# Decay and keys of the gated linear attention read from PSUM, the value gates multiplied in two halves, and the order of turns redrawn

## The reference

```python
# gla, H = 4 heads, 16 key and 32 value channels each
q = (x @ Wq); k = (x @ Wk); v = (x @ Wv)
gk = log_sigmoid(x @ gk_w1 @ gk_w2 + gk_b2) / 16
def step(S, qkvg):
    S = jnp.exp(gt)[..., None] * S + kt[..., None] * vt[..., None, :]
    ot = jnp.einsum('bhk,bhkv->bhv', qt, S)
# experts: the values are gated by expert and summed
xv = jnp.einsum('bsd,hedp->bshep', x, v_w)
v = jnp.einsum('bshep,bshe->bhsp', xv, gate_v)
```

## Time and profile before

| | before |
|---|---|
| median of 3 runs | 1421.68 us (1418.91 to 1423.92) |
| the profiled execution | 1440.95 us, span 1439.6 us |
| busy: TensorE, VectorE | 1271.5 us (88%), 1019.2 us (71%) |
| busy: ScalarE, GpSimd | 738.1 us (51%), 675.4 us (47%) |
| mean granted TensorE clock | 0.951 |

### The profile page before, as it was taken

How to read it: one execution, slowest core, us unless ns; L and a number is a source line. 1 busy time by engine, 2 the same in 40 slices (tenths; PEclk the granted TensorE clock), 3 DMA queues, 4 the chain that set the end, 5 groups by cost and what they waited for, 6 DMA issues and landing times.

```text
span 1439.6 us, 43040 instructions
## 1 busy us (share of the span) xinstructions
PE 1271.5 (88%) x18034; PEld 1014.5 (70%) x18034; DVE 1019.2 (71%) x2038; ACT 738.1 (51%) x2084; POOL 675.4 (47%) x549
## 2 busy tenths in 40 slices
PE   5576877999989999799999899979998899979887
PEld 3353566877777678578777778857787688867775
DVE  4758778877796877767688877887667676755334
ACT  5577865656554572445665367425673246323111
POOL 3445436673463446455556354445625464333500
PEclk9799989999999999999999999999999899989998
DMA  5101064743466347356566456744556465545642
GB/s 195 45 16 63 1 200 132 240 144 131 145 196 222 102 146 249 105 173 200 193 200 191 130 180 212 221 146 154 173 168 197 145 227 196 172 170 199 240 132 79
DMA packets 90721, 231.43 MB, mean 161 GB/s; under 512 B 9377, under 2 KB 15649, under 8 KB 90401
## 3 DMA queue, kind: packets, MB, share of 16 engines
q1 hardware_dynamic: 90384, 228.09, 48.6%
q10 hardware_dynamic: 144, 0.59, 0.1%
HBM read 225.50 MB, written 3.15 MB: 159 GB/s over the span
## 4 chain that ended last, share of the span: by engine, by line
PE 43%; DVE 10%; issue 3%; ACT 1%; DMA 1%; POOL 1%; DVEq 0%; ACTq 0%; POOLq 0%
PE bank L968 10%; PE bank L921 9%; PE bank L831 5%; PE bank L958 3%; PE bank L939 2%; PE bank L616 2%; DVE kv L1154 2%; PE bank L949 1%; PE bank L932 1%; PE bank L651 1%; PE bank L675 1%; DVE dy L1238 1%; DVE ogate L1401 1%; PE bank L711 1%; PE bank L661 1%
## 5 line engine op out<-in xcount | busy, mean ns | idle before, releaser
L1795 POOL TENSOR_TENSOR vgate<-vgate,xT 128x1024 f32<-128x1024 f32 x128 | 309.1, 2419 | 149.8 <-DMA vgate<-gates 149.6
L921 PE MATMUL bank<-wv,vgate 128*128 128x128 f32 x2048 | 261.5, 283 | 0.5 <-DVE state L1354 0.3
L921 PEld LDWEIGHTS bank<-wv,vgate 128*128 128x128 f32 x2048 | 251.0, 198 | 9.7 <-issue 3.9
L968 PE MATMUL bank<-ogate,wo 128*128 128x256 f32 x1024 | 254.1, 393 | 2.7 <-DVE ogate L1401 2.6
L968 PEld LDWEIGHTS bank<-ogate,wo 128*128 128x128 f32 x1024 | 195.5, 197 | 37.0 <-issue 10.6
L1401 DVE TENSOR_TENSOR ogate<-ogate,bank 128x1024 f32<-128x1024 f32 x128 | 153.4, 1209 | 37.5 <-PE bank L958 31.6
L1758 POOL TENSOR_TENSOR kv<-kv,gqk 128x512 f32<-128x512 f32 x64 | 84.8, 1326 | 125.0 <-DVE kv L1154 125.0
L1690 ACT ACTIVATE mprob<-bank,mmin 128x256 f32<-128x256 f32 x128 | 59.3, 469 | 138.7 <-DVE mmin L1390 138.5
L1512 ACT ACTIVATE prob<-prob,mx 128x128 f32<-128x128 f32 (+1 forms) x256 | 95.9, 376 | 57.7 <-DVE mx L1095 57.0
L1741 POOL TENSOR_TENSOR rot<-rot 128x512 f32<-128x512 f32 x64 | 83.5, 1305 | 86.1 <-DVE rot L1071 85.9
L1753 POOL TENSOR_TENSOR prob<-prob,rsum 128x256 f32<-128x256 f32 (+1 forms) x64 | 60.4, 943 | 130.7 <-DVE rsum L1098 130.5
(11 more groups left out here) (236 smaller groups left out, 2602.1 us busy)
## 6 DMA issues: line engine op xcount, KB each, us to landing
vgate<-gates SPq DMA_DIRECT2D x128, 512.0 KB, 4.3
ogate<-gates SPq DMA_DIRECT2D x128, 512.0 KB, 4.5
wv<-in_wv_moe SPq DMA_DIRECT2D x128, 256.0 KB, 4.6
wo<-in_wo_moe SPq DMA_DIRECT2D x128, 256.0 KB, 4.8
kv<-values SPq DMA_DIRECT2D x128, 128.0 KB
local<-in_local SPq DMA_DIRECT2D x1, 1715.0 KB, 9.6
wqkv<-in_wqkv SPq DMA_DIRECT2D x2, 768.0 KB, 6.5
x<-in_x SPq DMA_DIRECT2D x8, 128.0 KB, 7.9
```

What stands on the lines that cost most here:

```text
L921: i = nc.tensor.matmul(out[:, n * D:(n + 1) * D], xg[:, e, n * P:(n + 1) * P], m.wv[slot][:, e, :], start=(q, n, e) == (0, 0, 0), stop=(q, ...
L968: i = nc.tensor.matmul(out[:, 0:T], m.wo[slot][:, e, :], cg[:, e, :], start=(h, q, e) == (0, 0, 0), stop=(h, q, e) == (MH - 1, 1, EQ - 1))
L1795: tt(gate, gate, spread(m.xT[b % 2][:, :], 1, EQ), ALU.mult).then_inc(s.vgated, 1)
```

## The change

- `gqk` on ScalarE copies only the queries, to a tile `gq`. The keys stay in the bank.
- `gkv` on VectorE takes the keys from the bank. It waits for the decay instead of for the bank's release.
- The last step of `gz` on ScalarE writes the decay into the first half of that same bank, over the queries that have been copied out; it waits for that copy.
- `gmul` on VectorE reads the decay from the bank. Behind its last round the bank is released, by a semaphore instruction that waits for those scans. The bank is thus held from `gqk` to the last scan.
- `vgate` on GpSimd issues two instructions on 128x512 in place of one on 128x1024; the semaphore rises behind the second.
- All five tables of turns and the table of banks are drawn anew, with as many steps as before.

```diff
@@ VectorE
         v.wait_ge(s.kv_in[slot], 32 * use)
-        v.wait_ge(qk.emptied, qk.use)
-        v.chain(tt(kv[:, :, :], kv[:, :, :], spread(m.gqk[:, 1, :], 1, 2), ALU.mult))
+        v.wait_ge(s.gdecay, nth("gz", b))
+        v.chain(tt(kv[:, :, :], kv[:, :, :], spread(filled(qk)[:, T:2 * T], 1, 2), ALU.mult))
 
     def gmul(b, j):
-        kv = m.kv[kv_of(b, j)[0]]
+
+        kv, qk = m.kv[kv_of(b, j)[0]], banks.of("gqk", b)
         v.settle()
         v.wait_ge(s.gdecay, nth("gz", b))
         for n in range(2):
-            i = nc.vector.tensor_tensor_scan(kv[:, n, :], m.ge[:, :], kv[:, n, :], 0.0, ALU.mult, ALU.add)
+            i = nc.vector.tensor_tensor_scan(kv[:, n, :], qk.ap[:, 0:T], kv[:, n, :], 0.0, ALU.mult, ALU.add)
         i.then_inc(s.gscan, 1)
+        if j == GJ - 2:
+            v.wait_ge(s.gscan, nth("gmul", b, j))
+            nc.vector.sem_inc(qk.emptied, 1)
@@ ScalarE
     def gqk(b):
         bank = banks.of("gqk", b)
-        act(m.gqk[:, :, :], split(filled(bank), n=2), ACT.Copy).then_inc(bank.emptied, 1)
+        act(m.gq[:, :], filled(bank)[:, 0:T], ACT.Copy).then_inc(s.gq, 1)
...
         a.wait_ge(s.gmin, nth("gz", b))
-        act(m.ge[:, :], ge, ACT.Exp, scale=1.0 / 16.0).then_inc(s.gdecay, 1)
+        a.wait_ge(s.gq, nth("gqk", b))
+        act(banks.of("gqk", b).ap[:, 0:T], ge, ACT.Exp, scale=1.0 / 16.0).then_inc(s.gdecay, 1)
@@ GpSimd
-        tt(kv, kv, spread(m.gqk[:, 0, :], 1, 2), ALU.mult).then_inc(s.gmul, 1)
+        tt(kv, kv, spread(m.gq[:, :], 1, 2), ALU.mult).then_inc(s.gmul, 1)
...
-        tt(gate, gate, spread(m.xT[b % 2][:, :], 1, EQ), ALU.mult).then_inc(s.vgated, 1)
+        half = EQ // 2
+        for e in range(0, EQ, half):
+            i = tt(gate[:, e:e + half, :], gate[:, e:e + half, :], spread(m.xT[b % 2][:, :], 1, half), ALU.mult)
+        i.then_inc(s.vgated, 1)
@@ the third line of BANK_TURNS
-    "52736573726571316576523572135723156213523521572156315373523271537153715231623125321574271546713546317243617274"
+    "01501416046156051601016016540154065140652140625061562145615426142164242160240240624053045364526164564561245621"
```

More of the change, by code:

```diff
@@ L123 @@
[L123 to L128 removed]
+    "aaaaaaaaabbabaXGGGGbabbbaaabaabGaaabbbbbGcaabcbGbbbccbbGcGaabbabGaacaaacGGGbaGcbacbbcaaabbbGaabbGaaabbabbGbcab"
@@ new lines @@
+    "cbGbGbbcacbbaacabbzbGCcCaaAFGcaabbACGGabGccVacAVzVAAaAbbbPabPbbAbbaabaVcGVAAcVAaaFacaPAbFbAGPVAPVbACFVCaAaaPAA"
+    "DbGPbbAVbbPcbcVVAbbaAAbCaAcDaVADDcaGAADVADVDcaAGVDAADDAaPbbDAPDbDAaFPDDGAaaPADPDPDDGGGDAGVDDaPDVbbbbDDAcbbDAcD"
+    "DFbbDAFbDDacDAaaDDFGcDVDDVacaDaaaVVAADPPEAPbbDaGAVPAAVbAPPcADacDAbbbzAPbDGAbbVCPCDAbbPabGVcaCDDAAaDAPDDPFDAcaD"
+    "DaaGaVDDbbcGaVDaVbcDVDDAAGcPAPDGzGDDaFADaGFDDAADVDDAbDPbbDDPAbDbVDDVADAVDDAbDPbbVbFAcDDAAPAVEPVAPAAVADcPDDVDAC"
+    "DDAACcDAPDDaVDaaDDaGADDaaPDcDVDDaADaPDDVAcbDPDDbADCabDDGPDVDDAaVDAADDaVDbPDDbbPDbbbAaaVGbDbaAVbAAcAPacPVAGFAAc"
@@ new lines @@
+    "cAAVAcVcDPcPEzPADVPAAPADVPADDAACVAPDPDDACVDAAPDDAVPDFDDPDDACVDADADDADPDDPVDADDVDADDVDAPDDADPDDFDADDFVDAAFAVVPA"
+    "DDAAPAPEDADAADAVDPADPAADPADVDADPAADPADPDAVDDPVDVADAPPDDADVDDDADDADAVPDDAPDVDDADADDAPDADDVDVPADAPPE")
+VECTOR_TURNS = (
+    "VaaaaaaaaabaabbbaabGGaaGGaabGGGbaaGbGGaaGbGGcbbGGbcbcGGbbccccbGaaaaGcaacGaacbGGGbbcccGGcbbGGbaaGGaabGGabaGGGaa"
+    "abGGcbbGcbbcabbbccccazCaCGaacGCCCCCCCCbcabbcaGbAFaAaaGFccccVVzCFOAbaOAFbbGGbGGGGaaGGVVacaOcOVVAcACaabFObbaFbaG"
+    "GVVGAGAOFCCCFOFCbDCbDAOVVbACCbGDcccDGcGCVVGOaaAOAcaDaDDcOcDVVAADDaaVGDVDDAAbDbbObDDOFaFDOGDAaDAFDGODODFDGVbVbb"
+    "DObOccDcGGDcGDFAGDAFGGDacaDFcDaacDFGGDaDFaVDaaGGVVGEAGAbVDObbDObDDOAVGAGGVGcccDOcbzCabbCObADDAOaCCCCCCCCDcVVDD"
+    "OODaAaADDaaDcFDDcaFGabDbbGaDbFVDcccaVVVOOGcDFADAzCDCDFDFODODGAbDAGGbGDGDbVVGDbGODODVAVGGDADDFcDDDOOAEVAVFFODVV"
+    "ADcOAcDDDDDOaCDaOACADDVCDCVCaaDDaaCCDCDacDccaDGGDOOaVDabDcVGDbbDAGDbADDGGVDVODOGDbGDbDbDAbDAVaaVaOOcAaAccVVFOO"
+    "AaAaGFFbcccVVbbaObOGcaAFGAVVbEObbOVbAVaAaGGGGGcaaOOcFFAFcAGVGVGGaaOFObAVFbbAabDDDaVGcccGDcODzCOCADDAVVGaDGCCCC"
+    "OCbDDCbCCbOAbDVGAaGVGDDGDOODDcDaDAacDAVDaDcaDVOODFDFADGFDAaVaDVGDFDcOcDcODbGVDbbAVDbcADzCDaaGCOOVGEGAGVGbAGFFb"
+    "bFGbGGFFOOAVVcAcCCcCOCVCCDADAODaCcccDGCOcDaVGVAVGDADOGGDGaaGDDGODOaADDAaVVDDDOODAADDaDaDOVDVODbFDaDbAGaAbDFDbF"
+    "DOGVODVFDbaDabADaaGADbDaaVDbVaaOEOAAFVVbObbcObbFcbAcFbAFbcccVVcFGGOOGcGAGcAVcGDDDGVaacccOOcDVAzCDACGVGDDaCaCCC"
+    "OCCCCDOAGDDAVGaDVaGGGGDDOOVaDVbAabGADDGFDbODObVVDFDADAFDDOODbDVFDbAbDAGVDbDGOOAGVADFFVcDDFcDcDVFDAVAFccccEzCOC"
+    "DDODVVDOADADODVVAOADDDOCCCDVCVCODADCODACCDFDFFDDVODVODFADADDDDVDOVODDADADDDFFVDOADVFAODFFDDVDVOADAEDDDAOADOODD"
+    "ADAVVODDODOAADDODVDVODODADAVDVDDODODAADVDVDODDADODADVDOOE")
@@ new lines @@
+SCALAR_TURNS = (
+    "aaaaaaaaaaaabaaababXGGaGGaGbabbaaaaaaabbbaabbababacabbcbbcbcbabbGaGbbaabGaaaacaaacGGGaaacGabcbbabaaabbaaaababb"
+    "aabbababacaabbcbbcbabcbbaGbbGCabaCGaCcaaaAaFbCcGGbbcaaAGcAaaAaGCAaaFAbbbAbbbaAbbaFbaacaaAcaAaAcaFAababAFFFabCA"
+    "ACAaaaFAbbbAbcbAbaAbbaAbCaAaAcaAaacAAAcaAGGAaAaAbAbbaFDDGAAaAaGaGFAGaGFbbbbcbbAFbbaAbAaFFFAcaacaaFacaaDDaaAaEa"
+    "AAbaAbAbAAcAaAbCbbabbbACACAbbabcCaAAaAaFaAacaaGaGDDabcGabbcFAaaFAGAGCaFAaGAFFFGAbAbbAbbAbAbbDADbAcAEAAFAAAcAAC"
+    "ACacAAaaaaADaDaaacaaaAabCbbAaAAaAaabbbDbDbbAaAbbaAabAcAaAacaAFAcaAGAaGacbAaGbbAFaAaGAGaFEAaabbbAbbbaAGbbAGbaFa"
+    "AcaAacFFaAFAcaAAaaFbAabbAcAaaAaCAACACAaabbbCbbbAAbbAabAcDDaAaAacAaaFAcaGGAaFAGaaAcAFbGbbADGADaCAGaaAaEGaFAbbbA"
+    "FbbFFbACFbbAbAcACcAcAAAcAaACAaAAaaAaAAaAaaADDAAaAaaAFbaGGAaAbAabGFaAaaFabaabAbaaDaaADbaaaAbbEaAaabGAAFbAaGbbAb"
+    "cbbbcbFAcFFbcbbAFGbbAaGbAcAcAcAacAaACAaCACaAaaaCAAAaaAabAaAFDDAabAbaAAaAFAbbbGAbAGbbFAGbAbFAbAFFFcAcADDcFAcEAC"
+    "AAAAAACAAACAAFADDACFAFAAAAAAFAFFFADADAAFAEAAAAAAAAAAAAAAADDAAAAAAAAAADADAE")
@@ new lines @@
+GPSIMD_TURNS = (
+    "aaaaaaababaaGabGaGabaGaGaGbbGGbbaaaGaaaaabGGbbGaaGaaGabaGaaGbGbbbaaaGababWaWWaabbGWGWaWaaGaGaWabWabWGaGWDbWWbG"
+    "GWaaaaWWWWaWWabbaDGDDaDDDWbDbWDDGDDGGDaDaDaDaWaWaWGWaGDbbaGGWGWbbWaWaaaaWbaGDWDbWaWDDaDDDDDDWDbGDGDbGDDWGWWWDW"
+    "WWWaWaaDaaDDaDGWDaaDDbWDDbGDDGDDWDDbWWbGaaWaWaWWabaWabGaWWbbWaaGWaGaWGGaWababDWWGaWGWbWbGGWWDaDaDaDDaWDDDDWaDG"
+    "DWDaDWDDbWbaaWGWGbGbGWWWDWWGGWGaaGaWWaDDDWDaDaDDWDbaaDDDWbDDWGDaDaWaabaWaaWbabWbbWbWWGWGDGaWaWGaaWGaaGGWaWbWaG"
+    "WDbDDWDDWDDDDbWDDbDWGWDDDWWWWDWWWDDDDWDWDDWDDDDDDWDDWWDWWWWWDDWDDDWDDWDDDDWDDWDD")
@@ L145 @@
[L145 to L149, removed]
+    "01234567012346512734061527346152731523463175314753675143651741036574160351673452071360747236504372650243762453"
@@ L152 @@
+    "40652106542104520")
 PACKS = {
```

68 lines of the change are left out of this document (21 added, 47 removed).

## The result

| | before | changed |
|---|---|---|
| median | 1424.55 us, 6 runs | 1379.45 us, 6 runs (1373.33 to 1392.69) |
| ratio | | 0.9676, 95% interval 0.9642 to 0.9709 |
| profiled execution, span | 1439.6 us | 1391.4 us |
| mean granted TensorE clock, profiled | 0.951 | 0.960 |

The change makes the kernel 45 us faster, 3.2%. The prediction took 12 us off its 1421.68, to 1410 us, with a range down to 1386: right in sign and mechanism, and about a quarter of the size.

What follows compares the result with a forecast made beforehand. It took TensorE's own work as the bound, about a sixth of the chain waiting for VectorE. Gains of 29 + 6 = 35 us, six tenths kept (21), less 1 and 8, gave 12 us: median 1410 us, range 1386 to 1431.

Steps and rivals of the forecast that it cites:

- rival 4: Scans and products: reading the bank leaves scans blocked because kv is still in SBUF; 5 us more, 1427 us; chance 0.05.
- the port: Shared path where VectorE and GpSimd block each other; scans and products reading PSUM avoid it, 29 us before the discount.
- I keep six tenths: Whole sum: of 35 us gross only 21 show, as TensorE is nearly full; bounds three tenths and all.
- The share: Scans and products: part of blocked time on the path, 15 of 22 us late, 14 of 24 us early.
- The amount: Scans and products: blocked busy time beyond free durations, 22 us in the last 850 us, 24 us in the first 590.
- That is 6 us: Gate product in halves: shorter waits for VectorE lines L1238, L1194 and smaller ones gain 6 us, bounds 0 and 12.
- The bank: Bank held from L736 to the last scan: some takes wait, costing 8 us, bounds 0 and 42.
- The order: Redrawn tables of turns: may be some 8 us better or worse, taken as 0.
- GpSimd's longer gate products: Two halves of vgate on GpSimd: 23 us more GpSimd time, 1 us on the path.
- rival 3: Whole sum: all gain shows, no price for the bank, granted clock could stay higher; 34 us less, 1388; chance 0.2.
- Rival 1: Held bank becomes the wait, TensorE stops at take; slower, middle case 1432 us, at its bound 1443; chance 0.17.
- rival 2: Freed VectorE time turns into VectorE idle, TensorE having no room; no change, 1421 us; chance 0.15.

Runs made afterwards that it cites:

- e1: Redrawn tables of turns and banks alone under the old functions, against the kernel before: 1434.3 us, ratio 1.0047.
- e3: The changed kernel with the gate product in one instruction again (redrawn order and PSUM, no halves): 1395.2 us, 0.9782 of the kernel before.
- e5: e2 with the bank held until the last scan though nothing reads it after the copy: 1418.1 us, 0.9924 of the kernel before.
- e4: The changed kernel itself, run again beside the kernel before: 1380.5 us, ratio 0.9683.
- e8: The changed kernel plus one unused VectorE reduction over 640 columns in each of 64 rounds: 1396.3 us, 0.9778 of the kernel before.
- e13: The changed kernel plus unused work: 32 VectorE reductions of 2.2 us and 96 GpSimd memsets: 1416.2 us, 0.9900 of the kernel before.
- e14: e2 with the gate product in quarters instead of halves, decay and keys still in SBUF: 1398.5 us, 0.9801 of the kernel before.
- e2: The kernel before with redrawn order and gate product in halves, decay and keys in SBUF: 1415.0 us, ratio 0.9907.
- e7: The changed kernel with the gate product in quarters instead of halves: 1371.2 us, 0.9613 of the kernel before.
- e15: e7 with two other GpSimd products of 128x512 also split in two: 1382.0 us, 0.9680 of the kernel before.
- e9: The changed kernel plus 80 unused TensorE matmuls of 256 columns ahead of waits in six steps: 1399.2 us, 0.9789 of the kernel before.

## Why the prediction was wrong in size

**The mechanism** was right. A VectorE instruction with two SBUF inputs waits for a GpSimd instruction, one that reads a bank does not: 192 instructions lost their tail, rival 4 falls, and by e1, e3 and e5 it is the port and neither the order nor the bank that brings the gain. The condition was drawn too narrow, however. In the kernel before, the first convolution step (L1235) and a normalisation step (L1042) read only one full tensor from SBUF, beside columns of one element per partition, and have the same tail; the same line L1042 reading a bank has none:

```profile
L1235 DVE TENSOR_SCALAR dy<-pad,layer x24: 311/346/2410, 192.6 to 1262.4; 128x256 f32<-128x256 f32 x24
L1042 DVE TENSOR_SCALAR hn<-bank,lmv,lrstd x32: 384/401/410, 76.0 to 1216.2; 128x128 f32<-128x128 f32 x32
L1042 DVE TENSOR_SCALAR xn<-x,xmv,xrstd x16: 304/343/2384, 6.8 to 937.5; 128x128 f32<-128x128 f32 x16
```

The Trainium skill's rule in "SBUF — State Buffer", section "Who interferes with whom", frees instructions with at most one SBUF input only outside the 2-port modes, in which VectorE reads one input through two ports; the prediction left that condition out. The rule has another half that I did not use: the block goes both ways, depending on who starts first. The runs agree: GpSimd is busy 30 us longer with it (e5 against e4).

**PSUM as a source.** The median scan takes 665 ns on the bank and 691 in SBUF under the same order (e1), the fastest 643 and 645. The surcharge of an estimated 65 ns that the Trainium skill's "VectorE: DVE Perf Modes", section on the TRN2 errata, would give does not show, and was rightly left out.

**"I keep six tenths"**, the step that failed. On 35 us gross, the sum kept 21, and 17 of them for the port (29 × 0.6). What the port is worth by itself is 34 to 39 us, and 31 together with the order that it came with (e3 against before). Two things were mis-sized.

*The share.* I took one factor for the chain, 29 of 46 us, and a second one, six tenths, for other chains close behind: in all 17 of 46, a little under four tenths. The port passed on 34 to 39 us where VectorE's busy time fell by 59 to 64 and GpSimd's by 26 to 30: six tenths of VectorE's. The second discount should not have been there. Why the share is so high stays open in part. Evenly spread short pieces (e8) cost 14 of 37 busy us and e13's long ones 31 of 63, but with some 7 us of doubt on each difference the two shares can't be told apart.

*The amount.* I subtracted from busy time, which counts the overlap of neighbours once, the sum of free durations, which does not (56 × 0.680 and the like). The changed kernel shows what the free lines are busy, 80.8 us for the scans (its page) and 43.1 for the products (e4's groups), so that the excess before was 114.3 − 80.8 + 62.7 − 43.1 = 53 us and not 46. In the redrawn order, for which I counted nothing, it is 62 (e5: 124.2 and 61.5 us busy). And I counted nothing for GpSimd, which lost up to 30.

**"That is 6 us"**, for the halves: 15 us with decay and keys in PSUM, the case of the sum, 19 with them in SBUF, 12 in the old order. The two lines that I priced are not where it came from. From e3 to e4 VectorE's busy time falls by 15 us, of which `dy` has 0.5 (46.2 to 45.7) and `lc` 1.0 (9.4 to 8.4), where the sum had 9 for both; `dy` is held up more often and each time for less. The rest comes in 2 to 3 us each from lines that I had not priced, such as `dlt` (20.0 to 16.8), `do` (8.2 to 5.1) and `lsel` (8.3 to 6.1).

**The bank** was taken at 8 us and costs 3 by the medians (e5), which can be told neither from 0 nor from 8; its upper bound of 42 was far off, since no row was at hand to price it. **The order** was taken at 0 within 8 us either way and costs 6 to 7 alone (e1), inside the bound. **GpSimd's longer gate products** were taken at 1 us; e14 with 48 us more GpSimd time is still faster, so a small number was right.

**The clock.** It stood in rival 3 only, which at 1388 us came nearest to the result. Mean shortfall of the granted clock from full speed times the span is (1 − 0.952) × 1426.5 = 68 us before and (1 − 0.966) × 1379.2 = 47 us changed, in the timed runs of e1 and e4. This is an estimate of what the time at 1.2 GHz in place of 2.4 would cost a TensorE that worked all through it, and twice as long, 137 and 94 us, is spent at the lower level. So at most 21 of the 47 us between the two kernels are the clock's. Within the redrawn order the two kinds of gain mostly come together: from e1 over e2, e3 and e4 to e7 VectorE's busy time falls and the clock rises. But e15 breaks the row (932 us busy, 0.964), and e1 has more blocking than before and no lower clock. e9, the only run that changed TensorE's idle time by itself, did not settle how much of the 21 us is cause and how much is the same wait counted again.

Of what the prediction said would show: scan and product within 30 ns of their median, held (672 and 665 ns for the scan). No maximum over 750 ns, 692. `dy` at most 1.8 us, 1.51. VectorE down by 50 to 65 us, 72. Rival 1 and rival 2, not seen.

## What to carry to other kernels

When one line has a median far below its mean and a worst case that is longer by just the length of another engine's instruction, price the whole of the blocking, on both engines and on every line with such a tail, and subtract like from like: busy time from busy time, durations from durations. Take one operand from PSUM, or make the blocker's instructions short; the second needs no new plan of banks and was worth 12 to 19 us here. Don't multiply two discounts: the share that the chain shows is one already, and here six tenths of VectorE's blocked time came back, where two discounts had left less than four.

## What the runs showed of the hardware

- Blocking goes, as a rule, by the single instruction: dividing a GpSimd product of 128x1024 into four raised its time from 2.37 to 4 × 0.73 us and still took 36 us off the kernel with decay and keys in SBUF (e1 to e14). An exception stands in e15: `lc` waited out four quarters in a row, 2.78 us.
- The same program varies with its granted clock: of the changed kernel's six runs the one at 0.960 took 1391.4 us in span, the one at 0.971 1372.0.
- Scans on a bank are no slower than in SBUF: 665 against 691 ns in the median, 643 against 645 at the fastest.
- Two inputs in SBUF are not needed for a block: a normalisation step on one SBUF tensor takes up to 2384 ns where its median is 343, and reading a bank never more than 410 (L1042, before).
